# A hand-planned two-layer kernel: the planner's rank tables emptied, and the shared experts' sums kept in head 13's key memory

## The reference, cut to what matters

```python
x = L0_attn_x                                   # (2, 512, 256)
xn = _layernorm(x)
s = _L0_attn_ref(xn, w_qkv, b_qkv, w_out, b_out)       # causal softmax, 16 heads
g = _silu(_L0_ffn_ref(xn, router_w, w1, w2, w3))       # 8 experts, top 2
x = x + s * g
xn = _layernorm(x)
s = _L1_attn_ref(xn, W_qkv, W_z, W_b, W_a, conv_w, dt_bias, A_log, norm_w, W_out)
g = _silu(_L1_ffn_ref(xn, Wsh_up, Wsh_down, Wrt_up, Wrt_down, W_router))
return x + s * g

def step(state, inp):                            # in _L1_attn_ref, for each token
    q_t, k_t, v_t, b_t, d_t = inp
    delta = (v_t - k_t @ state) * b_t
    state = state * d_t + outer(k_t, delta)
    return state, q_t @ state

shared_out = sum over 2 experts of gelu(x @ up) @ down       # in _L1_ffn_ref
routed_out = sum over the best 2 of 16 of p * (gelu(x @ up) @ down)
return shared_out + routed_out
```

## Time and profile before

| | us |
|---|---|
| median of 3 runs | 1294.34 |
| lowest and highest | 1285.93, 1298.04 |
| the profiled execution | 1290.69 |
| its span, first to last instruction | 1288.9 |
| mean granted TensorE clock | 0.972 of full speed |
| PE, DVE, POOL, ACT busy | 91%, 82%, 67%, 65% |

### The profile page before, as it was taken

One profiled execution on the slowest core, in us unless ns is written; L12 is line 12 of the kernel. 1 busy time (PEld: TensorE's weight loads), 2 busy tenths in 40 slices (PEclk: granted clock), 3 DMA queues, 4 the chain that ended last, 5 costly groups with the idle time before them and its releaser, 6 DMA issues.

```text
span 1288.9 us, 28774 instructions
## 1 busy us (share of the span) xinstructions
PE 1176.2 (91%) x9866; PEld 987.2 (77%) x9866; DVE 1062.3 (82%) x2365; ACT 841.6 (65%) x2393; POOL 869.4 (67%) x1101
## 2 busy tenths in 40 slices
PE   8899889788986999998999899989999999899996
PEld 7665446666875888887888888878788889788885
DVE  5797236968799899888989799888799898789778
ACT  4013643657765678776778767868777878587775
POOL 3123442657778887787887788875888797776636
PEclk9899979989998999999999999999999999999998
DMA  7942102224334637345646364545355563645342
GB/s 232 244 140 67 55 27 95 66 54 106 90 97 106 184 66 217 106 150 141 171 104 193 93 195 112 177 142 166 75 175 147 151 157 109 176 120 155 93 130 69
DMA packets 219493, 165.95 MB, mean 129 GB/s; under 512 B 103572, under 2 KB 186772, under 8 KB 219348
## 3 DMA queue, kind: packets, MB, share of 16 engines
q1 hardware_dynamic: 214612, 149.82, 41.9%
q0 software_dynamic: 4736, 14.29, 3.9%
HBM read 115.71 MB, written 48.16 MB: 127 GB/s over the span
## 4 chain that ended last, share of the span: by engine, by line
PE 39%; DVE 19%; POOL 10%; DMA 10%; issue 8%; ACT 7%; SPq 5%; DVEq 0%; POOLq 0%; another core or an unknown queue 0%; ACTq 0%
PE ps L1359 12%; DMA XYLM<-parked 4%; SPq L1305 4%; DVE yv L2168 3%; DMA WK<-in_WK 3%; PE ps L1757 3%; DVE KQ L2168 2%; PE ps L1421 2%; PE ps L1632 2%; PE ps L1694 1%; PE ps L1724 1%; PE ps L1710 1%; PE ps L1765 1%; PE ps L1467 1%; DVE Mp L2047 1%
## 5 line engine op out<-in xcount | busy, mean ns | idle before, releaser
L2576 ACT ACTIVATE XYLM<-ps 128x512 f16<-128x512 f32 x216 | 125.3, 600 | 54.7 <-PE ps L1667 54.0
L2168 DVE SCALAR_TENSOR_TENSOR yv<-ps,cw,yv 128x511 f32<-128x511 f32 (+2 forms) x192 | 142.8, 745 | 6.5 <-ACT yv L2512 2.7
L2168 DVE SCALAR_TENSOR_TENSOR KQ<-ps,cw,KQ 128x511 f32<-128x511 f32 (+2 forms) x192 | 140.6, 743 | 8.4 <-ACT KQ L2512 6.0
L1359 PE MATMUL ps<-XH,WVh 128*128 128x256 f32 (+1 forms) x384 | 134.6, 351 | 3.3 <-DVE O L2367 1.8
L1359 PE MATMUL ps<-XH,WVl 128*128 128x256 f32 (+1 forms) x384 | 123.6, 322 | 0.0
L1359 PE MATMUL ps<-XL,WVh 128*128 128x256 f32 (+1 forms) x384 | 123.5, 322 | 0.0
L2610 ACT ACTIVATE sq<-O 128x128 bf16<-128x128 f32 x256 | 79.4, 310 | 58.3 <-DVE O L2348 20.1
L2616 ACT ACTIVATE O<-O,small 128x128 f32<-128x128 f32 x256 | 82.6, 408 | 22.4 <-POOL small L2854 21.9
L2298 DVE TENSOR_TENSOR ZL<-ps,cst 128x256 f16<-128x256 f32 x192 | 77.7, 417 | 21.0 <-PE ps L1653 19.5
L2873 POOL TENSOR_TENSOR OGL<-O,OGH 128x512 fp32r<-128x512 f32 x62 | 81.1, 1308 | 5.2
L1359 PEld LDWEIGHTS ps<-XH,WVh 128*128 128x128 f32 x384 | 73.6, 192 | 8.2 <-DVE O L2367 1.9
(11 more groups left out here) (359 smaller groups left out, 4072.6 us busy)
## 6 DMA issues: line engine op xcount, KB each, us to landing
XYLM<-parked SPq DMA_DIRECT2D x56, 512.0 KB
RC<-crow SPq DMA_DIRECT2D x128, 128.0 KB
decayed<-PTE SPq DMA_DIRECT2D x64, 256.0 KB
PT<-decayed SPq DMA_DIRECT2D x64, 256.0 KB
parked<-LM SPq DMA_DIRECT2D x56, 256.0 KB
WV<-in_WV SPq DMA_DIRECT2D x16, 512.0 KB, 4.1
exr<-in_ex SPq DMA_DIRECT2D x16, 384.0 KB, 4.3
WK<-in_WK SPq DMA_DIRECT2D x16, 256.0 KB, 4.7
```

Of the source, the lines that this page charges most:

```text
L1359: m = pe.matmul(o, a, b, start=c + k == 0, stop=c == 1 and k == 2)
L2168: m = dve.scalar_tensor_tensor(out=dst[:, k:512], in0=ps[:, bk, 0:512 - k], scalar=cw[:, h, j, 3 - k:4 - k], in1=dst[:, k:512], op0=ALU.mu ...
L2576: leave(act.activation(changed(u, k), ps[:, bank("b", u, k), :].rearrange("p (c n t) -> p c n t", c=2, t=1 << (k - 1)), ACT.Copy), "b", u, k)
```

## The change

Three things change together.

1. `RANK` and `LATER` are empty, so that rank and start are those that the `plan_...` functions give, and `GRAIN`, the step by which starts count as equal, goes from 0.097 to 0.0517. Every engine's list changes. No computation is added or removed: PE, DVE and POOL have as many instructions of each kind as before. ACT has 34 loads of a function table in place of 31, since its pieces stand in another order.
2. The planner's costs of three pieces (`iv1`, `p8`, `q8`) rise. They are numbers of the planner alone.
3. `total` is now place 1 of `KQ`, that of head 13, and `WVh` a tile alone. `fld` waits for the last product that reads head 13's keys, `("KS", 55, b)`, in place of those of head 15.

```diff
 RANK = {
-    "KS": {"ACT": 216.88, "DVE": -218.39, "PE": -1070.92}, "KS:first": {"ACT": 260.06, "DVE": 361.08, "PE": 955.48},
...
 }
 LATER = {
-    "KS": {"ACT": 0.13}, "KS:first": {"ACT": 0.2, "PE": 0.11}, "KS:last": {"ACT": 0.5, "PE": 0.58},
...
 }
...
-    GRAIN = 0.09700
+    GRAIN = 0.0517
...
-    P.add(("iv1", h), rank + 0.1, ("DVE", 3.6, (("dg", h), "DMA"), (("xc", h - 1), "ACT") if h > LEAD else None,
+    P.add(("iv1", h), rank + 0.1, ("DVE", 3.9, (("dg", h), "DMA"), (("xc", h - 1), "ACT") if h > LEAD else None,
...
-    P.add(("p8", h), rank + 0.1, ("POOL", 1.15, (("iv1", h), "DVE")))
+    P.add(("p8", h), rank + 0.1, ("POOL", 1.55, (("iv1", h), "DVE")))
...
-    P.add(("q8", h), rank + 0.1, ("POOL", 1.15, (("iv2", h), "DVE")))
+    P.add(("q8", h), rank + 0.1, ("POOL", 1.6, (("iv2", h), "DVE")))
...
-    weights = [(("cv", h, v, b), "PE") for h in (HK - 2, HK - 1) for v in range(2) for b in range(2)]
-    weights += [(("Zt", h, n), "PE") for h in (HK - 2, HK - 1) for n in (0, 2, 4, 6)]
-    P.add(("fld",), 4 * HK - 8, ("SP", 6.0, *weights))
+    P.add(("fld",), 4 * HK - 8, ("SP", 6.0, *[(("KS", 4 * HK - 9, b), "PE") for b in range(2)]))
...
-        total, WVh = twins("total", "WVh", [128, 2, 2, 512])
-        total = total[:].rearrange("p a c n -> p (a c n)").rearrange("p (n d) -> p n d", n=NT)
+        WVh = sb("WVh", [128, 2, 2, 512], F32R)
...
+        total = KQ[:, (HK - 3) % 3].rearrange("p k t -> p (k t)").rearrange("p (n d) -> p n d", n=NT)
...
-                    for k in (HK - 2, HK - 1):
-                        for b in range(2):
-                            w.wait_ge(*full("cv", k, 0, b))
-                            w.wait_ge(*full("cv", k, 1, b))
-                        for n in range(0, NT, 2):
-                            w.wait_ge(*full("Zt", k, n))
+                    for b in range(2):
+                        w.wait_ge(*full("KS", 4 * HK - 9, b))
```

More of the change, by code:

```diff
@@ L109 @@
-    "kb:first": {"POOL": -118.76}, "kn": {"ACT": 143.35, "PE": -2619.8, "POOL": 47.57},
-    "kn:first": {"ACT": -11.62, "PE": -887.52, "POOL": -405.45}, "kns": {"ACT": 225.45},
-    "kns:first": {"ACT": -220.12}, "ld": {"DMA": -0.42, "SP": -1480.26}, "ld:last": {"DMA": -137.82, "SP": -123.41},
-    "ln1": {"PE": 271.7}, "ls": {"DMA": 958.97, "SP": -76.85}, "ls:last": {"DMA": 30.48, "SP": -41.47},
-    "mk:0": {"POOL": 24.4}, "nr2": {"DVE": 3.99}, "nrm": {"DVE": -207.98, "POOL": -183.54}, "oc:0": {"ACT": 303.06},
@@ L119 @@
-    "p1:1": {"DVE": -97.29, "PE": 154.63}, "p8": {"POOL": 370.67}, "pd": {"DMA": -718.47},
-    "pd:first": {"DMA": 160.16, "SP": 98.8}, "pd:last": {"DMA": -202.71, "SP": 23.4},
-    "pf": {"DVE": 394.78, "SP": 10.96}, "pl": {"POOL": -324.42}, "pl:first": {"POOL": 98.45},
-    "pl:last": {"POOL": 167.76}, "pm": {"POOL": -47.7}, "pre": {"ACT": -3.59, "DVE": 612.24}, "ps": {"SP": -7.82},
-    "ps:first": {"DMA": 4.29, "SP": 151.71}, "ps:last": {"DMA": -72.99, "SP": 1705.87}, "pt": {"DVE": 498.54},
@@ L155 @@
-    "dd:0": {"SP": 1.09}, "dec": {"POOL": 2.1}, "dec:first": {"ACT": 0.38, "POOL": 2.16}, "dec:last": {"POOL": 0.78},
-    "dg": {"DMA": 0.38}, "dn": {"DVE": 0.53}, "exd:0": {"DVE": 0.98}, "exd:1": {"DVE": 1.18}, "exg:0": {"ACT": 0.12},
-    "exg:1": {"ACT": 0.85, "DVE": 0.41}, "exv:0": {"DVE": 0.34, "PE": 0.14}, "exv:1": {"PE": 0.25},
-    "fO": {"POOL": 0.54}, "fV": {"POOL": 1.1}, "fWK": {"POOL": 0.01, "SP": 0.34}, "fWO": {"POOL": 2, "SP": 0.32},
-    "fWV": {"POOL": 3.49, "SP": 0.06}, "fin": {"DVE": 0.69, "SP": 2.61}, "fld": {"SP": 2}, "fs": {"ACT": 0.6},
@@ L160 @@
-    "fst": {"SP": 1.22}, "fup": {"POOL": 0.96, "SP": 1.13}, "fx": {"POOL": 3.01, "SP": 0.28}, "g0": {"ACT": 0.28},
-    "gg": {"DVE": 1.1}, "gram": {"DVE": 0.23}, "gram:first": {"PE": 0.01}, "gram:last": {"DVE": 0.95},
-    "gt": {"ACT": 0.16}, "hits": {"DVE": 1.67}, "iv1": {"DVE": 0.03}, "iv3": {"DVE": 0.23}, "kb": {"POOL": 0.43},
-    "kb:first": {"POOL": 0.58}, "kn": {"ACT": 0.38, "POOL": 2.48}, "kn:first": {"ACT": 1.02, "POOL": 1.96},
-    "ld": {"DMA": 0.02}, "ld:last": {"SP": 1.07}, "ln1": {"ACT": 0.85, "DVE": 0.13},
@@ L165 @@
-    "ls:last": {"DMA": 2.03, "SP": 2.26}, "mk:0": {"POOL": 0.9}, "mk:1": {"POOL": 0.75}, "nr2": {"DVE": 0.07},
-    "nrm": {"POOL": 2.04}, "oc:1": {"ACT": 0.42}, "on": {"ACT": 0.4}, "on:first": {"ACT": 0.35},
-    "on:last": {"ACT": 0.56}, "op": {"DVE": 0.71}, "os": {"POOL": 2.17}, "os:first": {"POOL": 0.41},
-    "os:last": {"POOL": 3.05}, "ot": {"DVE": 0.17}, "ot:first": {"PE": 0.06}, "ot:last": {"DVE": 0.38, "PE": 0.15},
-    "ov:1": {"DVE": 0.93, "PE": 0.95}, "own": {"DVE": 0.04}, "p1:0": {"DVE": 0.7, "PE": 0.02},
@@ L170 @@
-    "p1:1": {"DVE": 0.54, "PE": 0.02}, "p8": {"POOL": 0.03}, "pd": {"SP": 0.31}, "pd:first": {"SP": 0.11},
-    "pd:last": {"DMA": 2.22}, "pf": {"DVE": 0.67, "SP": 0.1}, "pl": {"POOL": 1.47}, "pl:first": {"POOL": 1.07},
-    "pl:last": {"POOL": 0.6}, "pm": {"POOL": 0.08}, "pm:first": {"POOL": 0.17}, "pm:last": {"POOL": 0.98},
-    "pre": {"DVE": 0.12}, "ps": {"SP": 0.45}, "ps:first": {"SP": 0.99}, "ps:last": {"DMA": 1.03, "SP": 1.88},
[3 rows of a table removed]
-    "sc:1": {"ACT": 0.5}, "sd": {"DVE": 0.15}, "slot": {"DVE": 0.08}, "small": {"SP": 0.53}, "so": {"DVE": 0.04},
@@ L183 @@
-    "xr": {"SP": 2.24}, "xs": {"SP": 1.5}, "y": {"PE": 0.07}, "y:last": {"DVE": 0.78, "PE": 0.04},
-    "yl:last": {"DVE": 1, "PE": 0.08},
 }
```

50 lines of the change are left out of this document (removed), and 17 rows, old and new, of tables (LATER, RANK).

## The result

The changed kernel takes 1280.56 us (median of 20 runs, 1274.37 to 1285.59), the kernel before in the same session 1290.09 us (median of 20 as well; one of them took 6312.19 us, which nothing here explains). The ratio is 0.9919, with a 95% interval of 0.9897 to 0.9941: 0.8% faster, where 1310 us and 1.2% slower was forecast. The profiled execution took 1281.08 us.

A forecast was written before the change was run, and what follows sets the result against it. The prediction took a nearly full PE, with DVE not far behind, as the bound. Its terms, -8 + 4 - 4 + 3 + 2 + 15 + 1 = +13, plus 3 for smaller places, took 1294.3 to 1310 us; range 1281 to 1336.

The forecast's parts named there:

- the outputs' term: Each chunk's output product now stands right behind its DVE and POOL chain, so late POOL results cost PE +15 us.
- the planner's costs: Raised costs of iv1, p8 and q8 in the planner: the prediction gave them no term and no rival.
- Under 5 shows it wrong: Sign for PE's waits for POOL at the OGH and OGL products: some 15 us confirms, under 5 refutes.
- The end: Last stretch: the shared experts' sums leave it, freeing DVE and ending POOL's 10.8 us wait; -8 us.
- the additions: The sums' DVE additions, moved five chunks earlier, meet little idle time there and take back +4 us.
- Routed experts earlier: The first routed group moves into the first chunks (300 to 400 us) and fills PE's idle time; -4 us.
- Layer 0's sums: Layer 0's attention: fewer masks cover the sums' trip through memory, so POOL stalls and PE waits for masks; +3 us.
- the prologue: Choosing the routed experts, 4.2 us of DVE, now stands ahead of `pre` 3 and delays that chain; +2 us.
- Table loads: Three more function-table loads on ACT, 1.283 us each; +1 us.
- The steady part: From 400 to 1200 us: PE idle for 55 to 65 us was forecast, against 46.6 before.
- Rival 1: Outputs' margin suffices, the end gives 9.5 us and the first chunks 8: 1278 us, 1.3% faster; chance 0.16.
- Rival 3: Outputs lose 1 us each, or additions and mask stalls hold PE at their upper bounds: 1350 us; chance 0.07.

The follow-up runs named there:

- e2: The changed kernel without the move of the shared experts' sums into head 13's key memory: 1282.33 us, ratio 0.9909 to the kernel before.
- e3: The changed kernel with the old GRAIN of 0.097: 1285.59 us, ratio 0.9938 to the kernel before.
- e7: The changed kernel with the three planner costs (iv1, p8, q8) as before: 1294.7 us, ratio 1.0038 to the kernel before.
- e12 to e15: The changed kernel at GRAIN 0.0450 (raised costs 1.0012, old costs 1.0136) and 0.0400 (raised 1.0026, old 1.0080), as ratios to the kernel before.
- e18: The changed kernel with GRAIN 0.0861 and rank 62 for the gathers and additions at the end: 1272.35 us, ratio 0.9823 to the kernel before.
- e8: One extra, unused POOL cast ahead of each cast to OGH: 1301.52 us in the kernel before, 1296.93 us in the changed one.
- e1: The kernel before with only the move of the shared experts' sums into head 13's key memory: 1304.59 us, ratio 1.0088.
- e19: The kernel before, tables and GRAIN kept, with only the three planner costs raised: 1403.52 us, ratio 1.0847.

## Why the prediction was wrong, step by step

The forecast was +16 us and the runs show -10. Two steps failed, and each is over half of the 26 us between: the outputs' term (+15, measured +1) and the planner's costs, priced at nothing (measured -15 in these lists). The smaller terms make up the difference. The forecast started from a median of 1294.3; that of the 20 runs is 1290.1, and this adds 4 us to its distance.

- **The planner's costs.** This step failed. The prediction took them as numbers of the planner alone, priced them at nothing and gave no rival to them, though the products' 1.52 and 1.58 us stood in the trace beside the 1.15 and 1.55 of the diff. They are worth 7 to 16 us at three grains, 12.8 on average. Without them the emptied tables measure 1.0038, 1.0136 and 1.0080, that is 5 to 18 us slower. That the forecast was 16 is no support for it: its main term, the outputs, isn't what these orders lose.
- **The outputs, +15.** This step failed too, in size. PE's waits for `OGH` and `OGL` went from 3.5 + 0.8 to 1.8 + 3.6 us, so +1. "Under 5 shows it wrong", the prediction said; it is 5.4. In the other kernels with empty tables (e2, e3, e7, e12 to e15, e18) they are 1.5 to 10.4 us, with old costs or raised ones. The margin is thin (28 of 62 late with 0.62 us less, e8), so the mechanism was there. The error was the size: one chunk in three or four losing 1 us came from no row, while the rows of the same kind that the prediction names stood at 1 to 4 us each. Measured are five waits.
- **The end, -8, and the additions, +4.** Wrong in size, and the rows that would show it came true without paying: POOL's wait for an addition is down from 10.8 us to 1.5, DVE is busy for 26.0 of the last 39 us (35.1 before), and its wait for the load of the sums is 0.6 us (forecast: near 1). But PE is idle there for 10.0 us as before, not 5 or less. The additions delay head 15's inverse by 7.5 us. In sum the move gives nothing in this order; it wins 6 us in e18's and costs 12 in the old lists.
- **Routed experts earlier, -4.** PE's idle time from 300 to 400 us is 13.3 against 16.4; 12 had been forecast.
- **Layer 0's sums, +3, the prologue, +2.** Both small: PE's idle time is 13.0 against 12.6 us from 100 to 220 us, and 12.9 against 14.1 from 220 to 300, so +0.4 and -1.2. POOL's wait for the inverted sums, forecast near 10 us, is 18.9 up to 215 us, as before, and PE's wait for masks went down from 9.0 to 6.4. The 2 us that the prediction gives from the Trainium skill (DMA: Bandwidth & Descriptors, section Anatomy of one DMA) are stated there for DMAs that POOL issues, and these are SP's.
- **Table loads, +1.** Not told apart by any run.
- **The steady part.** The prediction saw in it only what could go wrong at the outputs, and had no term for what a fresh greedy order wins elsewhere. The wait for `XYLM<-parked` fell by 9 us in this order and rose in two others. That part looks like the luck of one order: four values of `GRAIN` with the same costs spread over 1.1%, and the changed kernel has the best of the four.
- **Rival 1.** It had 1278 us, 2.6 us from the median, and its first premise held, that the outputs' margin suffices. But it took 9.5 us from the end and 8 from the first chunks, and they gave nothing and 3. Its number is near by luck.
- **Slips in its sums.** The 12 additions among chunks 56 to 58 are 7.1 us; 9.5 us are all 16. Rival 3 speaks of 1 us for each chunk and reckons with 0.7 (43 us; at 1 it would be 62). Neither changes the forecast.

What stays open: why one of these orders meets the loads of the inverse in time and the next doesn't. And DVE's wait for `PR` isn't the measure of the time by itself: e18 has 17.7 us of it and is the fastest. Nor is the 12 us loss of e1 explained, or why e18's order keeps a higher clock.

## What to carry to other kernels

Where a static order is made from a cost model, the costs are part of the kernel: compare each edited cost with the duration in the trace before calling it free, since an engine behind a piece that is longer than planned can wait in many of its repetitions (15 of 28 in e7). Corrections fitted to wrong costs are tied to them (e19 was 8.5% slower), so they are taken out or refitted together with them. And judge a rule for the order by several orders that it gives; here four orders of one rule spread over 1.1%.
